# A fused attention and feed-forward kernel: last stage's first scales and tiles made one stage earlier, its last batch normalised by VectorE, bias rows awaited later, and idle products at three stage ends

## The reference

```python
x = x + tanh(g_xattn[0]) * attention(layernorm(x), ctx)        # 16 heads, rope, softmax, projection
x = x + tanh(g_ffn[0])   * experts(layernorm(x))               # router, top 2 of 8, and a shared MLP
x = x + tanh(g_xattn[1]) * coattention(layernorm(x), ctx)      # similarities, softmax, features @ W_qv
x = x + tanh(g_ffn[1])   * bitffn(layernorm(x))

def bitffn(x):                                                 # inner width 1024
    gate = silu(bitlinear(x, w_gate)); up = bitlinear(x, w_up)
    return bitlinear(gate * up, w_down)

def bitlinear(x, w):       # act_quant: scale = 127 / clip(max |row|, 1e-5), round, divide by the scale
    return act_quant(x) @ weight_quant(w).T
```

## Time and profile before

| | |
|---|---|
| three timed runs | 738.36, 742.09, 738.27 us; median 738.36 us |
| profiled execution | 739.67 us, of which the profile spans 737.9 us |
| mean granted clock of TensorE | 0.946 |
| busy: TensorE | 653.4 us (89%) |
| busy: VectorE | 454.3 us (62%) |
| busy: ScalarE | 340.9 us (46%) |
| busy: GpSimd | 314.9 us (43%) |

### The profile page before, as it was taken

How to read it: one execution, slowest core, us unless ns; L and a number is a source line. 1 busy time by engine, 2 the same in 40 slices (tenths; PEclk the granted TensorE clock), 3 DMA queues, 4 the chain that set the end, 5 groups by cost and what they waited for, 6 DMA issues and landing times. The chain is left out here.

```text
span 737.9 us, 9674 instructions
## 1 busy us (share of the span) xinstructions
PE 653.4 (89%) x3270; PEld 408.0 (55%) x3270; DVE 454.3 (62%) x774; ACT 340.9 (46%) x598; POOL 314.9 (43%) x490
## 2 busy tenths in 40 slices
PE   4995799999999878789999999996799999957985
PEld 2661343434334247466777777773667676833553
DVE  4787688888888237487343434435475464358994
ACT  2464388888888863454322223423221212012665
POOL 8667568586544407500010100101232626356897
PEclk9997599999999999899999999998999899986999
DMA  8379866746300058003000000001000000000001
GB/s 266 132 251 278 162 61 86 88 52 86 46 1 1 1 199 314 14 1 113 16 1 0 1 0 0 1 0 57 1 0 1 1 1 0 1 0 1 31 33 51
DMA packets 23144, 43.41 MB, mean 59 GB/s; under 512 B 4060, under 2 KB 10848, under 8 KB 22336
## 3 DMA queue, kind: packets, MB, share of 16 engines
q1 hardware_dynamic: 15224, 31.02, 12.5%
q0 software_dynamic: 6048, 10.03, 10.5%
q10 hardware_dynamic: 1832, 1.84, 1.1%
HBM read 32.27 MB, written 10.49 MB: 58 GB/s over the span
## 5 line engine op out<-in xcount | busy, mean ns | idle before, releaser
L714 DVE TENSOR_REDUCE mx<-ps_f 128x2 f32<-128x1024 f32 x128 | 151.4, 1220 | 30.3 <-PE ps_f L652 30.0
L817 ACT ACTIVATE prob<-ps_s 128x512 f32<-128x512 f32 x256 | 134.6, 607 | 34.1 <-PE ps_s L670 34.1
L670 PE MATMUL ps_s<-q_stacks,k_stacks 53*128 53x512 f32 x256 | 90.2, 483 | 5.8 <-ACT prob L817 3.3
L670 PEld LDWEIGHTS ps_s<-q_stacks,k_stacks 53*128 53x128 f32 x256 | 35.8, 188 | 87.0 <-ACT prob L817 70.9
L652 PE MATMUL ps_f<-k_stacks,q_stacks 53*128 53x512 f32 x256 | 64.7, 456 | 9.7 <-PEq L209 5.2
L679 PE MATMUL ps_o<-prob,vst 128*32 128x512 f32 x512 | 69.0, 612 | 0.0
L174 POOL TENSOR_TENSOR norm_tmp_att<-st 128x4 f32<-128x4 f32 x4 | 1.0, 242 | 145.3 <-DVE st L1339 145.3
L1300 DVE SCALAR_TENSOR_TENSOR h<-ps_u,most,qs 128x512 f32<-128x512 f32 x32 | 24.0, 751 | 62.7 <-ACT qs L1230 62.7
L1230 ACT ACTIVATE qs<-ps_g 128x512 f32<-128x512 f32 x40 | 23.9, 597 | 82.4 <-PE ps_u L1102 82.4
L741 POOL TENSOR_TENSOR q_stacks<-minus,q_stacks 128x1024 fp32r<-128x1024 f32 x16 | 38.0, 2375 | 37.8 <-ACT minus L808 37.8
L1760 ACT ACTIVATE qs<-ps_SC,nmax 128x512 f32<-128x512 f32 x16 | 11.0, 687 | 68.8 <-DVE nmax L1648 68.8
(11 more groups left out here) (298 smaller groups left out, 1467.7 us busy)
## 6 DMA issues: line engine op xcount, KB each, us to landing
k_stacks<-room_k POOLq DMA_DIRECT2D x18, 256.0 KB, 5.9
q_stacks<-room_q POOLq DMA_DIRECT2D x18, 256.0 KB, 5.5
up<-in_up SPq DMA_DIRECT2D x10, 256.0 KB, 6.6
x<-in_x SPq DMA_DIRECT2D x4, 512.0 KB, 10.1
ctx_raw<-in_ctxTC SPq DMA_DIRECT2D x4, 512.0 KB, 6.7
room_k<-k_high SPq DMA_DIRECT2D x4, 512.0 KB, 5.0
room_k<-k_low SPq DMA_DIRECT2D x4, 512.0 KB, 6.3
room_q<-q_high SPq DMA_DIRECT2D x4, 512.0 KB, 5.6
```

Source lines behind the costliest of these rows:

```text
L670: pe.matmul(ps_s[n % 3][:, :], ks[rows(h), 2 * s + pair, kt * P:(kt + 1) * P], qs[rows(h), 2 * s + pair, :], start=True, stop=True).then_i ...
L714: dve.tensor_reduce(mx[:, f % 2, qt, 2 * pair:2 * pair + 2], ps_f[n % 2][:, :, :], AX_X, ALU.max).then_inc(used, 1)
L817: act.activation(prob[:, kt % 2, j, :], ps_s[n % 3][:, :], ACT.Exp, scale=SCALE)\
```

## The change

It has four parts.

1. **Scales and tiles.** The buffers and semaphores of scales and rounded tiles are made before coattention. At coattention's end VectorE makes the scales of batch 0 ahead of the last four residuals, and GpSimd makes tiles 0 and 1. In the last stage VectorE makes the scales of batch 1 behind its first copy, those of batches 2 and 3 behind `hidden(0)` and `hidden(3)`.
2. **Normalisation.** The last batch's statistics stay on GpSimd, behind tile 2. Its two passes over four tiles go, and VectorE makes one pass (`normalise_late`) behind `hidden(1)`.
3. **Bias rows.** In attention `split(0)` and `lower(0)` stand ahead of `coef` and the wait for the bias rows.
4. **Idle products.** TensorE multiplies the 128x128 float32 identity by itself into a PSUM bank that is free, 14 times at preparation's end, 16 at projection's and 9 at the experts'. Nobody reads the results.

```diff
+def idle_products(pe, out, square, count):
+    for _ in range(count):
+        pe.matmul(out, square, square, start=True, stop=True)
...
                 queries(b)
+            pe.wait_ge(parts, 2 * B - 1)
+            idle_products(pe, ps_k[0][:, 0:P], id32, 14)
...
             stage_values(1, 1)
+            split(0)
+            lower(0)
             pool.tensor_tensor(coef[:, :], per["mask"][:, :], per["gates"][:, 0:1].broadcast_to([P, T]), ALU.mult)\
                 .then_inc(coef_done, 1)
             pool.wait_ge(coef_done, 1)
             pool.wait_ge(bp_in, 16)
-            split(0)
-            lower(0)
...
             project(B - 1)
+            idle_products(pe, ps_t[0][:, 0, :, :].rearrange("p j c -> p (j c)"), id32, 16)
...
             y_transposes(B - 1)
+            idle_products(pe, ps_g[0][:, 0:P], id32, 9)
...
             batches(dve, batch, weight_means)
+            dve.tensor_scalar(early["gd"][:, 0:1], wstat[:, 2:3], per["gates"][:, 3:4], 1.0 / 127.0, ALU.mult, ALU.mult)
+            batch_scales(dve, early, ffn, xn, wstat, 0)
             for q in range(QT):
                 residual(B - 1, q)
...
+            for n in range(2):
+                quantise(pool, early, xn, n, n)
...
-            quantise(0, 0)
-            quantise(1, 1)
-            normalise_batch(pool, per, ffn, B - 1)
             for n in range(T + 3):
                 if live(n + 2):
-                    quantise(n + 2, n % 2)
+                    quantise(pool, early, xn, n + 2, n % 2, xT_done)
+                if n == 0:
+                    batch_statistics(pool, per, ffn, B - 1)
                 if live(n - 1):
                     rounded(n - 1, 1 - n % 2)
...
                     hidden(n, u)
-                if isinstance(n, int) and 0 <= n < B - 1:
-                    scales(n + 1)
-            dve.tensor_scalar(gd[:, 0:1], wstat[:, 2:3], per["gates"][:, 3:4], 1.0 / 127.0, ALU.mult, ALU.mult)
-            scales(0)
+                if isinstance(n, int) and n == 0:
+                    batch_scales(dve, early, ffn, xn, wstat, 2)
+                if isinstance(n, int) and n == 1:
+                    normalise_late(dve, per, ffn, B - 1, ffn["normed"])
+                if isinstance(n, int) and n == 3:
+                    batch_scales(dve, early, ffn, xn, wstat, B - 1)
             transposed(0, 0)
+            batch_scales(dve, early, ffn, xn, wstat, 1)
             schedule(dve, step)
```

More of the change, by code:

```diff
@@ L1801, in _, with phase_bitffn @@
                     quantise_weights(b)
-def phase_bitffn(nc, per, ffn, xn, free, wq16, wstat, out):
+            for n in range(2):
+                quantise(pool, early, xn, n, n)
+def phase_bitffn(nc, per, ffn, xn, free, wq16, wstat, early, out):
     x_sb, c16 = per["x"], per["c16"]
@@ L1837, in phase_bitffn @@
         block = ctx.enter_context(nc.Block())
-        ABS, AMAX, INV, SX, AG, AU = range(6)
         @block.sync
@@ L2121, in build @@
                 ffn = batch_norm_state(nc, ctx, "_ffn", lambda t: xn[:, t, :])
+                early = scales_state(nc, ctx)
                 phase_coattend(nc, a, per, att_norm, ffn, free, room, ctok, ctxT, wqv, w32, wabs, wq16, wstat,
-                               arrived["context"], arrived["weights"], arrived["magnitudes"], small)
+                               arrived["context"], arrived["weights"], arrived["magnitudes"], small, early, xn)
                 if stop > 3:
-                    phase_bitffn(nc, per, ffn, xn, free, wq16, wstat, out)
+                    phase_bitffn(nc, per, ffn, xn, free, wq16, wstat, early, out)
         if stop <= 3:
```

68 lines of the change are left out of this document (38 added, 30 removed).

## The result

| | before | changed |
|---|---|---|
| median of four runs beside each other | 739.01 us | 729.21 us |
| all runs | 738.27 to 742.09 us | 728.03 to 730.53 us |
| profiled execution, and its span | 739.67, 737.9 us | 729.56, 727.3 us |
| mean granted clock | 0.946 | 0.957 |

The medians differ by 9.8 us, where 11.8 (from 738.36 to 726.6) were forecast. The measured ratio is 0.9841, 95% interval 0.9803 to 0.9878; it would give 11.8 us less, and the quotient of the two medians, 0.9867, lies in its interval. By that interval the gain is 9.0 to 14.6 us. The predicted range of 722.5 to 731.5 us holds the time.

A forecast was written before the change was run, and what follows sets the result against it. The last stage was taken as a chain of waits, attention as a full TensorE starting late. Terms 2.7 + 2.0 + 0.5 + 7.3 = 12.5 us off the profiled 739.67, shifted towards the median, gave 726.6 us, range 722.5 to 731.5.

The forecast's parts named there:

- Bias rows, 2.7 (1.3 to 3.2): Attention's opening: the first split no longer waits for the bias rows, starts 2.7 us earlier, and attention carries the gain.
- Price of an idle product, 0.25 us (0.24 to 0.45): Stage ends: 14, 16 and 9 products take 3.5, 4.0 and 2.3 us; only the 16 overrun, by about 0.4 us.
- the slower rival: Stage ends: idle products at 0.9 us each overrun their covers by 24.4 us, total 753; decides from 0.53 us; chance 0.02.
- Experts' opening, 2.0 (0 to 2.8): Experts' opening: idle products hold TensorE's upper level, saving 2.3 us less 0.4 overrun, taken as 2.0.
- the choice between row and rule: Stage openings: trace row shows clock 1.00 under transposes; the skill's rule would put terms 2.0 and 0.5 near 0; row chosen.
- Coattention's opening, 0.5 (0 to 0.6): Coattention's opening: upper level could gain 2.4 us, but ScalarE is free only at 511.94, so 0.5 us.
- Preparation, 0: Preparation's end: the 14 products gain nothing, since reductions set attention's pace until 76 whatever the level.
- Last stage, 7.3 (4.8 to 8.3): Last stage: VectorE's chain of 27.4 us lets GpSimd round tile 4 at 681.0, not 689.06; 8.1 us less 0.8.
- Rival 3: Last stage: VectorE slowed further by GpSimd beside it, stage gives only 3 to 4 us, total about 730; chance 0.05.
- I take 0.8 off: Last stage: allowance for a stretch at TensorE's lower level, mostly hidden under tiles 0 to 2, later up to 3.3 us.
- no change: Whole kernel: no change within the measurement, for instance bias gain lost to the clock and coattention's falls unlucky; chance 0.02.
- Level kept through attention's opening: Attention's opening: the 14 products keep TensorE's upper level, 4 us more gained, total 722.5; chance 0.06.

The follow-up runs named there:

- the six-product kernel: The changed kernel with six idle products added at coattention's end, ahead of the last stage: 729.33 us, ratio 0.9833.
- the part alone: The kernel before with only the changes of scales, tiles and normalisation (parts 1 and 2 of the change): 733.48 us, ratio 0.9907.

## Why the prediction was right, and where it was off

**Bias rows, 2.7 (1.3 to 3.2).** Right: the split is 2.9 us earlier, with no DMA as its releaser. The profiled run of the changed kernel carried all 2.9, which was luck. The prediction named what could eat it, the return of the level. With the bias edit and the same work behind it (without the runs that add products in attention or have a fall at its end), attention took:

| level returns after the stage's start, us | 23.7 | 24.6 | 24.6 | 28.8 | 29.2 | 29.5 | 29.8 |
|---|---|---|---|---|---|---|---|
| attention, us | 197.97 | 198.33 | 198.35 | 199.99 | 200.02 | 200.32 | 200.22 |

Without the edit the level returned at 26.9 to 27.5 and attention took 201.2 to 201.4 us. The mean with the edit is 199.3 us, so the edit is worth 2.0 us on the mean of these, not 2.7. Why the return comes at 24 us in some runs and at 29 in others is open.

**Price of an idle product, 0.25 us (0.24 to 0.45).** 0.233 to 0.24 us at the three stage ends, at the upper level; so no overrun, where 0.4 was expected. In attention's opening, at the lower level, a product took 0.79 us, alone between two pairs of first scores. That is above the 0.53 from which the slower rival decides. In a row the price is lower even at that level. The nearest row is that of the 16 transposes of 128 columns which open the experts before the change, at 0.50:

```profile
300.75 3.73 PE L1082 MATMUL ps_xE<-c,qs 128*128 128x128 f32 x16 [3.92 <-PEq L847]
```

Two such records make a product, so 0.47 us as an estimate. The stage ends do not lie at that level anyway.

**Experts' opening, 2.0 (0 to 2.8).** 2.25 in the profile. The experts took 200.6 us in all eleven profiles with the 16 products, and 202.6 to 202.8 in the three without. The term holds, and with it the choice between row and rule. In the experts' opening the transposes run at 1.00 in the changed kernel, as those of projection did in the earlier trace rows. The Trainium skill ("TensorE: Matmul & The Clock Gate", Part 4: PE-mode transpose) has it that transposes do not count as busy like products; this trace does not bear that out. A stretch of transposes can still be at the lower level: in the six-product kernel above those of projection ran at 0.50, after a stretch in which TensorE was busy 1.55 us between 261.4 and 264.8. But there they also brought the level back. TensorE does nothing but transposes in this stage until its first product at 272.82, and the level has returned at 271.64:

```profile
268.20:271.60 3.40, 3.25 (x16) 2.88 (x15) 0.79 (x3) 1.89 (x4) 0.00 (x0) 0.50 1.00 392
271.70:272.80 1.10, 0.94 (x8) 0.73 (x8) 0.92 (x4) 0.89 (x2) 0.00 (x0) 1.00 1.05 404
```

The kernel without the 14 and the 9 products shows the same (0.50 until 273.14, first product at 274.32).

**Coattention's opening, 0.5 (0 to 0.6).** The first exponential comes 8.63 us after the stage's start in nine of the ten profiles with the 9 products (8.47 in the tenth, where the level does not fall in the opening), 8.88 before the change and 9.25 in the three others without them: 0.25 to 0.6 us earlier, as bounded. The stage as a whole took 149.2 to 151.7 us in ten profiles with the products and 150.2 to 152.2 in four without. The means differ by 1.0 (149.96 and 150.93), less than the scatter, and the profile's 0.95 proves nothing. The 2 us allowed either way were needed.

**Preparation, 0.** Right as a term: with the three groups of products alone attention took 201.4 us, 201.2 before. What the 14 products move is the fall: 0.3 to 3.2 us into attention in the ten profiles with them, between 1.2 us ahead of its start and 0.15 behind it in the four without.

**Last stage, 7.3 (4.8 to 8.3): the step that failed.** The profile gave 3.8. The mechanism stands: VectorE's chain up to tile 4, GpSimd's own pace from there. The size of its terms was wrong: the chain took 30.9 us, not 27.4, against which 0.8 had been taken off, and GpSimd's pace behind it 49.4 us, not 48.8 (3.5 - 0.8 + 0.6 = 3.3 us of the 3.5 that the term is short).

- "The normalisation 1.4": it took 3.06 or 3.07 in all seven profiles that have it behind the second hidden product, 1.63 ahead of the first, where GpSimd has only small instructions, and with it on ScalarE the chain is 27.1 us. The price was read at 304.08, where no GpSimd rounding runs. Rival 3 had this mechanism with 0.05; its forecast of a stage that gives 3 to 4 us and 730 us in all is what came. The Trainium skill ("SBUF — State Buffer", Who interferes with whom) says that VectorE in some modes and GpSimd take an exclusive lock on a shared pair of ports, so that the later one stands still. The rows agree as far as they go: of VectorE's TENSOR_SCALAR instructions on 4 or 256 columns each that grew ended just behind GpSimd's, and ScalarE's, which by that page has its own ports, do not grow. No run here shows the ports themselves.
- "TensorE ... should open at the upper level" and "I take 0.8 off": it fell to the lower level within 1 us in both profiles of the changed kernel, and that costs 1.4 us (80.3 to 80.45 against 78.95 to 79.1). Of VectorE's wait of 1.54 us, 0.3 stays without the fall; the sum had no wait at all.
- "scales of batches 2 and 3, 2.8 each": those of batch 3 took 3.6 us in the changed kernel, by the same wait of VectorE's small instructions for GpSimd's.

Against which stage of before one measures matters too: the old last stage took 84.15, 84.05 and 86.11 us in three profiles of the same code. So by the profiles the part is worth 3.6 to 7.2 us, and 7.3 lies just above that. The ratio of the part alone says 6.9 (4.2 to 9.5), with 7.3 inside; it also holds what the other stages did. That the total came out inside the range is partly luck: the other stages together gave 1.6 us more in this profile than was forecast, against the missing 3.5.

**Sum.** 11.8 forecast; 9.8 measured by the medians, 11.8 by the ratio, and by the ratios of the parts 3.0 + 2.0 + 6.9 = 11.9. **Slower by overrun, and no change:** both out, by the price of 0.233 us at the stage ends and by the interval. **Level kept through attention's opening:** out; two kernels with TensorE busy all through, or nearly so, did not get it back. The Trainium skill ("TensorE: Matmul & The Clock Gate", Part 1) has a busy TensorE come back to the upper level; the 27 us without a gap at 0.50 are against it in this place (busy as the profile models it).

## What to carry to other kernels

Take the price of a VectorE instruction from a row where the same neighbours are busy: a pass that moves from GpSimd to VectorE and then runs beside GpSimd may cost twice its time alone, because instructions of some forms are not done before GpSimd's are; ScalarE may be the better place for it. This holds for instructions on four numbers as well. Idle products held the clock where a short pause stood between dense work and a dense opening, but not where the work behind is thin, and as float32 fillers in attention's opening they were a cost. When one kernel's clock changes level at other places from run to run, compare stages over several profiles of the same code before giving a difference of 2 us a cause.

## What was not expected of the hardware

- With TensorE busy for 27.2 of 27.2 us (float32 products on 53 rows, between them float32 products on 128), the granted clock stayed at 0.50 and returned only at 91.1; with bf16 fillers it returned at 92.1.
- VectorE's float32 pass of 256 columns took 0.40 to 1.20 us beside GpSimd's rounding, its TENSOR_SCALAR on four numbers up to 1.00 us instead of 0.20, and each that grew ended 0.02 to 0.17 us after a GpSimd instruction; ScalarE's on 256 columns stayed at 0.42.
- TensorE's level came back to 1.00 at 271.64, in the kernel with six products at coattention's end, with nothing but transposes since the stage's start.
- The same program had attention of 198.3 and 200.0 us and coattention of 149.2 and 151.7 us in two profiles, by where the level changed.
